# Vision tower on one core: who prepares the constants between embedding and the first attention pass

## The reference, cut to what matters

```python
def fake_quant(x, n_bits=8):
    qmax = 127
    scale = max(max(abs(x)) / qmax, 1e-8)      # one scale for the whole tensor
    return clip(round(x / scale), -128, 127) * scale
h = tokens(x)                                   # 64 x 197 x 192
y = layernorm(h)
qkv = fake_quant(y) @ fake_quant(w_qkv).T + b_qkv
attn = softmax(fake_quant(q) @ fake_quant(k).T * 16 ** -0.5)
out = fake_quant(attn) @ fake_quant(v)
h = h + fake_quant(out) @ fake_quant(w_proj).T + b_proj
h = h + experts(layernorm(h))
```

## Time and profile before

| What | us |
|---|---|
| median of 3 runs (lowest, highest) | 2035.22 (2034.53, 2038.62) |
| the profiled execution, its own time | 2038.77 |
| its span | 2037.0 |
| busy: PE / DVE / ACT / POOL | 1492.0 / 1433.1 / 1379.6 / 1164.9 |
| prologue of `normalise`, first instruction to `turn(1)` | 285.56 to 311.72 |
| loop of `normalise` | 311.72 to 422.6 |
| epilogue and barrier | 422.65 to 428.9 |
| start of `attend_maxima` to its first matmul | 428.91 to 435.21 |

### The profile page before, as it was taken

How to read it: one execution, slowest core, us unless ns; L and a number is a source line. 1 busy time by engine, 2 the same in 40 slices (tenths; PEclk the granted TensorE clock), 3 DMA queues, 4 the chain that set the end, 5 groups by cost and what they waited for, 6 DMA issues and landing times. The chain is left out here.

```text
span 2037.0 us, 50049 instructions
## 1 busy us (share of the span) xinstructions
PE 1492.0 (73%) x12152; PEld 987.7 (48%) x12153; DVE 1433.1 (70%) x3551; ACT 1379.6 (68%) x3956; POOL 1164.9 (57%) x1903
## 2 busy tenths in 40 slices
PE   6999957855656556563688885888864999994563
PEld 6999954411111111111344443554434988884553
DVE  2545559977777777777466666888876777774996
ACT  1323224429999999997799995777662766663885
POOL 2333330046666666663356552577775788884997
PEclk9999978965555555555555555555556999996886
DMA  7654410002222222221554545444434555554785
GB/s 293 256 233 191 163 39 1 1 28 87 83 74 74 76 86 81 76 74 52 124 151 138 151 139 153 137 155 154 151 120 116 134 139 144 145 145 143 224 270 158
DMA packets 184912, 262.77 MB, mean 129 GB/s; under 512 B 28372, under 2 KB 147363, under 8 KB 180328
## 3 DMA queue, kind: packets, MB, share of 16 engines
q1 hardware_dynamic: 137456, 202.16, 32.0%
q0 software_dynamic: 19840, 39.17, 5.4%
q10 hardware_dynamic: 27540, 20.52, 3.1%
HBM read 149.17 MB, written 108.01 MB: 126 GB/s over the span
## 5 line engine op out<-in xcount | busy, mean ns | idle before, releaser
L947 ACT ACTIVATE exps_summed<-s,neg_shift 128x197 f32<-128x197 f32 x1184 | 482.7, 479 | 33.9 <-POOL neg_shift L814 32.7
L984 DVE TENSOR_REDUCE score_max<-s 128x788 f32 (+2 forms) x320 | 284.7, 893 | 107.7 <-PE s L888 95.0
L947 ACT ACTIVATION_READ_ACCUMULATOR exps_summed<-s,neg_shift (+1 forms) x1184 | 304.9, 260 | 0.0
L1346 ACT ACTIVATE exps<-st,scalars 128x788 f32<-128x788 f32 (+1 forms) x320 | 246.4, 889 | 15.4 <-PE st L1255 15.4
L2027 POOL DMA_INDIRECT expert_sums<-y_tile,row_places x216 | 215.5, 998 | 60.3 <-issue 25.6
L367 PE MATMUL mm<-w_tok,x_transposed 128*128 128x192 f32 x1176 | 209.5, 329 | 0.8 <-ACT x_transposed L328 0.8
L888 PE MATMUL s<-k_int,qk_int 16*128 16x197 bf16 x768 | 98.8, 355 | 138.6 <-ACT exps_summed L947 123.4
L328 ACT COPY x_transposed<-tp 128x768 f32<-128x768 f32 x98 | 78.1, 798 | 176.9 <-PE tp L359 176.9
L367 PEld LDWEIGHTS mm<-w_tok,x_transposed 128*128 128x128 f32 x1176 | 190.9, 192 | 1.2 <-ACT x_transposed L328 1.2
L350 POOL TENSOR_SCALAR x_patches<-x_tile 128x768 f32<-128x768 f32 x98 | 81.4, 831 | 188.0 <-PE tp L359 172.2
L1166 POOL TENSOR_SCALAR probs<-exps 128x788 bf16<-128x788 f32 (+1 forms) x160 | 130.0, 819 | 102.5 <-ACT exps L1346 102.4
(11 more groups left out here) (416 smaller groups left out, 4506.1 us busy)
## 6 DMA issues: line engine op xcount, KB each, us to landing
x_tile<-in_x SPq DMA_DIRECT2D x21, 1792.0 KB, 11.0
z_tile<-listed_rows SPq DMA_DIRECT2D x108, 196.0 KB
v_ints<-v_slots SPq DMA_DIRECT2D x32, 480.0 KB
v_slots_in<-v_ints SPq DMA_DIRECT2D x32, 480.0 KB, 3.7
q_ints<-qk_int SPq DMA_DIRECT2D x32, 295.5 KB
k_ints<-k_int SPq DMA_DIRECT2D x32, 295.5 KB
q_shifted<-q_ints SPq DMA_DIRECT2D x32, 295.5 KB, 3.6
k_ones<-k_ints SPq DMA_DIRECT2D x32, 295.5 KB, 4.2
```

Source lines behind the costliest of these rows:

```text
L947: act.activation(gone[:, v % 2, k], ps[v % 3][:, k, 0:SEQ], ACT.Exp, scale=alpha, bias=nb[:, s, to:to + 1], accum_out=p.lsum[:, bass.ds(n ...
L984: dve.tensor_reduce(columns(m, u), src, op=ALU.max, axis=AXL.X).then_inc(max_done, 1)
L1346: act.activation(ex[:, v % 4, 0:size(u)], src, ACT.Exp, scale=alpha, bias=p.col(C_LNSA)).then_inc(e_ready, 1)
```

## The change

1. POOL takes over, behind its fill of ones in `normalise`: the six instructions on the bias row (after waiting for `rows_ok` and the loads), then, after `b_mv` and a new semaphore `cw_ok`, the five copies of weight slots, the two broadcasts into `kk`, and the four clears that stood at the start of `attend_maxima`.
2. The six maxima of the weights (L559 to L564) move behind the rows' chain on DVE.
3. The sum that gives `C_ONES` moves from the epilogue to the start of DVE's stream.
4. PE runs `turn(0)` ahead of the transposes of the weights, DVE runs `spread(0, 0)` ahead of the copies out of PSUM, and PE waits for `b_mv` itself before the loop.
5. `masks` counts to 3 and `zero` to 1. The five tiles are allocated outside of `attend_maxima`.

```diff
@@ normalise, gpsimd
                 pool.memset(x1[D1:KB], 1.0).then_inc(ones_ok, 1)
                 pool.wait_ge(ones_ok, 1)
+                link = make_link(pool, bch)
+                pool.wait_ge(rows_ok, 1)
+                pool.wait_ge(ld, 80)
+                link(pool.tensor_scalar(brow[:], brow[:], p.col(C_IX, 0, 1), p.col(C_IW, 0, 1), ALU.mult, ALU.mult))
+                link(pool.tensor_copy(bpart[:, 0], brow[:]))
+                link(pool.tensor_tensor(bres[:], brow[:], bpart[:, 0], ALU.subtract))
+                link(pool.tensor_copy(bpart[:, 1], bres[:]))
+                link(pool.tensor_tensor(bres[:], bres[:], bpart[:, 1], ALU.subtract))
+                link(pool.tensor_copy(bpart[:, 2], bres[:]))
+                pool.sem_inc(b_in, 1)
+                pool.wait_ge(b_mv, 48)
+                pool.wait_ge(cw_ok, 1)
+                for to, w in ((p.wslot0, cw0), (p.wslot1, cw1)):
+                    for t in range(2):
+                        link(pool.tensor_copy(to[:].rearrange("p g a w -> p (g a) w")[:, :, HD * t:HD * t + HD],
+                                              w[:, t * D:(t + 1) * D].rearrange("p (s d) -> p s d", d=HD)))
+                link(pool.tensor_copy(p.wv0[:], cw0[:, 2 * D:3 * D]))
+                for k in range(2):
+                    pool.tensor_copy(p.kk[:, k].rearrange("p g t -> p (g t)"),
+                                     p.col(C_ONES).broadcast_to([128, GRP * 2 * SEQ])).then_inc(laid, 1)
+                for v in (p.lq, p.xl0, p.xl1, p.vs):
+                    pool.memset(v[:], 0.0).then_inc(laid, 1)
+                pool.wait_ge(laid, 6)
@@ normalise, tensor
                 spread_maxima(nc, p, bank, 3, red)
+                def turn(t):
+                    ...
+                turn(0)
                 pe.wait_ge(w_ok, 1)
...
-                turn(0)
                 pe.wait_ge(w_ok, 2)
                 pe.wait_ge(ones_ok, 1)
+                pe.wait_ge(b_mv, 48)
@@ normalise, vector
                 link(dve.memset(mx[:], 0.0))
+                slots = p.idf[:].rearrange("p (h s) -> p h s", s=SLOT)
+                link(dve.reduce_sum(p.col(C_ONES), slots[:, :, HD:HD + 3], axis=AXL.XY))
...
-                dve.wait_ge(ld, 80)
-                (six maxima of the weights)
                 dve.wait_ge(chain_a, 2)
                 (the rows' chain)
+                dve.wait_ge(ld, 80)
+                (six maxima of the weights)
                 dve.sem_inc(max_ok, 1)
...
-                dve.sem_inc(w_ok, 1)
-                (six instructions on the bias row)
-                dve.sem_inc(b_in, 1)
-                dve.wait_ge(w_t, 1)
-                (six copies out of PSUM)
-                dve.wait_ge(b_mv, 48)
-                (five copies into slots)
                 dve.sem_inc(w_ok, 1)
+                spread(0, 0)
+                dve.wait_ge(w_t, 1)
+                (six copies out of PSUM)
+                dve.sem_inc(cw_ok, 1)
+                dve.sem_inc(w_ok, 1)
@@ attend_maxima
-                sp.wait_ge(masks, 5)
+                sp.wait_ge(masks, 3)
...
-                pool.memset(lq[:], 0.0).then_inc(zero, 1)
-                pool.memset(xl0[:], 0.0).then_inc(zero, 1)
-                pool.memset(xl1[:], 0.0).then_inc(zero, 1)
                 pool.tensor_copy(na[:], p.col(C_NALPHA).broadcast_to([128, 4])).then_inc(zero, 1)
-                pool.memset(vs[:], 0.0).then_inc(zero, 1)
-                pool.wait_ge(zero, 5)
-                pool.wait_ge(masks, 5)
+                pool.wait_ge(zero, 1)
+                pool.wait_ge(masks, 3)
...
-                for s in range(2):
-                    dve.tensor_copy(kk[:, s].rearrange("p g t -> p (g t)"),
-                                    p.col(C_ONES).broadcast_to([128, GRP * 2 * SEQ])).then_inc(masks, 1)
-                dve.wait_ge(masks, 5)
+                dve.wait_ge(masks, 3)
```

More of the change, by code:

```diff
@@ L432, in normalise @@
         (ld, chain, chain_a, red, w_t, w_ok, b_in, b_mv, y_ready, t_done, x_ready, cls_t,
-         q_done, q_max, red2, eps_ok, max_ok, rows_ok, ones_ok, tick_t) = p.sems(
+         q_done, q_max, red2, eps_ok, max_ok, rows_ok, ones_ok, cw_ok, laid, bch, tick_t) = p.sems(
             p.early, "b", "ld chain chain_a red w_t w_ok b_in b_mv y_ready t_done x_ready cls_t "
-            "q_done q_max red2 eps_ok max_ok rows_ok ones_ok tick_t")
+            "q_done q_max red2 eps_ok max_ok rows_ok ones_ok cw_ok laid bch tick_t")
         DOUBLES = ([((q, j), (q, j + 1)) for q in range(PAIRS) for j in (0, 2)]
@@ L489, in _ @@
                 spread_maxima(nc, p, bank, 3, red)
+                def turn(t):
+                    b = t % 2
+                    pe.wait_ge(y_ready, t + 1)
+                    need(pe, x_ready, t - 1)
+                    for u in range(2):
+                        nc.tensor.transpose(pa[b][:, u, 0:ROWS], y[:, b, u, 0:128], p.idf[0:ROWS, 0:ROWS])
+                        done = nc.tensor.transpose(pa[b][0:D1, 2 + u, 0:ROWS], y[:, b, u, 128:D], p.idf[0:ROWS, 0:ROWS])
+                    done.then_inc(t_done, 1)
+                turn(0)
                 pe.wait_ge(w_ok, 1)
@@ L504, in _ @@
                 last.then_inc(w_t, 1)
[L506 to L513, removed]
                 def channels(g, d):
@@ L578, in _ @@
                 link(dve.tensor_tensor(pm[0:ROWS, 0:1], pm[0:ROWS, 0:1], cst[0:ROWS, 11:12], ALU.max))
+                dve.wait_ge(ld, 80)
+                link(dve.tensor_reduce(pm[:, 1:2], w_rows[:, 0:4, :], op=ALU.max, axis=AXL.XY, apply_absolute_value=True))
+                link(dve.tensor_reduce(cst[0:64, 12:13], w_rows[0:64, 4, :], op=ALU.max, axis=AXL.X, apply_absolute_value=True))
+                link(dve.tensor_tensor(pm[0:64, 1:2], pm[0:64, 1:2], cst[0:64, 12:13], ALU.max))
+                link(dve.tensor_reduce(pm[:, 2:3], w_tail[:, 0, :], op=ALU.max, axis=AXL.X, apply_absolute_value=True))
+                link(dve.tensor_reduce(cst[0:64, 13:14], w_tail[0:64, 1, :], op=ALU.max, axis=AXL.X, apply_absolute_value=True))
+                link(dve.tensor_tensor(pm[0:64, 2:3], pm[0:64, 2:3], cst[0:64, 13:14], ALU.max))
                 dve.sem_inc(max_ok, 1)
@@ L637, in spread @@
                     ins.then_inc(x_ready, 1)
+                spread(0, 0)
+                dve.wait_ge(w_t, 1)
+                pw = pq[:].bitcast(BF16)
+                link(dve.tensor_copy(cw0[:], pw[:, 0, 0:3 * D]))
+                link(dve.tensor_copy(cw1[0:D1, :], pw[0:D1, 1, 0:3 * D]))
+                link(dve.tensor_copy(p.wp0[:], pw[:, 2, 0:D]))
+                link(dve.tensor_copy(p.wp1[0:D1], pw[0:D1, 3, 0:D]))
+                link(dve.tensor_copy(x0[:, :, 0:1], pw[:, 4, 0:1].rearrange("p (a b) -> p a b", a=1).broadcast_to([128, B, 1])))
+                link(dve.tensor_copy(x1[0:D1, :, 0:1], pw[0:D1, 4, 128:129].rearrange("p (a b) -> p a b", a=1).broadcast_to([D1, B, 1])))
+                dve.sem_inc(cw_ok, 1)
+                dve.sem_inc(w_ok, 1)
                 def maxima(g, d):
@@ L647, in _ @@
                     for w2 in range(SIDE // 2):
-                        spread(g, w2)
+                        if g or w2:
+                            spread(g, w2)
                         if g:
@@ L905, in scores @@
                     ins.then_inc(s_ready, 1)
-                pe.wait_ge(masks, 5)
+                pe.wait_ge(masks, 3)
                 for g in range(GRP):
@@ L2391, in build @@
             p.cw1 = far("w_qkv1", [KB, 3 * D], BF16)
+            p.kk = far("k_int", [128, 2, GRP, 2 * SEQ], BF16)
+            p.lq = far("q_ends", [128, 2, 2, GRP * STAMP], BF16)
+            p.xl0 = far("x_ends0", [128, 2, 256], BF16)
+            p.xl1 = far("x_ends1", [KB, 2, 256], BF16)
+            p.vs = far("v_slots", [128, 2, VW], BF16)
             normalise(p)
```

14 lines of the change are left out of this document (1 added, 13 removed).

## The result

| kernel | median us (lowest, highest) | against before, 95% interval |
|---|---|---|
| before, 4 runs beside it | 2035.42 (2034.53, 2038.62) | |
| after, 4 runs | 2050.08 (2049.00, 2050.62) | 1.0063 [1.0050, 1.0076] |

The change costs about 14.7 us where 4.3 us of gain were forecast; the time lies outside the range of 2026 to 2034 and on the other side of the old kernel.

The account below looks back on a forecast made before the run. Gains were sought around the normalisation's DVE-busy loop: DVE's chain ahead, PE waiting for DVE's broadcasts behind. 5.9 us behind less 1.6 ahead gave 4.3; 2035.22 - 4.3 = 2030.9 us, range 2026 to 2034.

Parts of the forecast that it names:

- The later stages start at barriers and shift as a whole.: Stages behind the first attention pass: the 4.3 us gain was to carry through to the kernel's end.
- D: Rival, normalisation loop: POOL's work holds DVE's spreads, making the kernel slower, up to 2040 us; chance 6%.
- Masks and clears: Behind the normalisation loop: PE starts attention 5.7 us sooner and the late sum saves 0.2 us, 5.9 in all.
- Held by the fill: Prologue: POOL's fill holds L199 until 296.16, leaving 0.86 of 2.26 us; row factors at 298.34 instead of 299.20.
- Bias: Prologue: POOL's bias work takes turns with DVE's rounding, which ends at 307.25 instead of 303.51.
- cheap bound: Prologue: POOL's first bias instruction priced from 0.68 us instead of 1.8; rounding ends at 306.15, gain 5.4 us.
- turn(1): PE's step at the end of the prologue: starts at 313.3 instead of 311.72, 1.6 us later.
- The added wait for: PE ahead of the normalisation loop: bias lands at 309.0, so the wait costs nothing, with 4 us of cover.
- C: Rival, prologue: POOL stalls at first use, so PE's bias wait comes last; gain 2.5 us, 2032.7; chance 17%.
- POOL's slots, broadcasts and clears in the loop: Normalisation loop: some 9.5 us of POOL work costs zero; up to 9 us if that fails.
- A: The forecast: DVE and POOL take turns in the prologue; gain 3 to 6 us, 2029.2 to 2032.2; chance 62%.
- Local sum: Normalisation: 5.9 us gained behind the loop less 1.6 lost ahead of it, 4.3 us.

Follow-up runs that it names:

- Experiments 1 and 2: experiment 1, and the kernel before with 28 embedding row maxima taken in pairs, 14 DVE instructions fewer: 2055.55 us, ratio 1.0086.
- experiment 1: The kernel after with 14 one-column memsets on DVE ahead of its first wait in the embedding: 2033.94 us, ratio 0.9986.
- -14: DVE's projection loop 14 places earlier than before: the kernel after, 2050.08 us, and the kernel before with 14 DVE instructions fewer, 2055.55 us.
- +114: The kernel before with 114 one-column memsets on DVE in the embedding, loop 114 places later: 2055.53 us.
- -20: The kernel after with 12 embedding row maxima taken in 6 pairs, loop 20 places earlier than before: 2036.25 us.
- -11: The kernel after with 3 one-column memsets on DVE in the embedding, loop 11 places earlier than before: 2033.98 us.
- -7: The kernel after with 7 one-column memsets on DVE in the embedding, loop 7 places earlier than before: 2036.24 us.
- 0: DVE's projection loop at its old place: the kernel before, 2035.42 us, and the kernel after with 14 memsets, 2033.94 us.

## Why the prediction was wrong

The step that failed is its last one: "The later stages start at barriers and shift as a whole." They start at barriers, but the time that they take isn't fixed if the instructions ahead of them have changed in number. Taking 14 instructions off DVE's stream was counted by their durations alone; it also moved the projection's loop onto a bad place, at 22.0 us in that stage. Experiments 1 and 2 show that this count alone switches the loss off and on. None of the rivals had it: D, the slower one, sat in the normalisation (POOL holding spreads), and L637's spreads there last 431 to 478 ns (432 to 476 before), with DVE as busy in the loop as before (78.38 against 78.46).

The other steps, against the trace:

- *Masks and clears:* 5.7 + 0.2 foreseen behind the loop; the loop ended 0.44 later and PE started 5.48 sooner, 5.92.
- *Held by the fill:* L199 was to end at 296.2, it ended at 296.08; row factors at 298.34 foreseen, at 298.22 found.
- *Bias:* the first instruction was taken at 1.8 us from its nearest row (L753) and took 0.81. With it the rounding was to end at 307.25; with the cheap bound, 306.15. It ended at 305.93. Here the size was off, not the mechanism. The waiting was DVE's almost alone, though (3.4 us of it against 0.4 on POOL).
- *turn(1):* 1.6 later foreseen with the dear price, 0.5 with the cheap one, 0.38 found.
- *The added wait for* `b_mv`*:* not last; PE's idle before `turn(1)` was ended by DVE's `w_ok`. C falls.
- *POOL's slots, broadcasts and clears in the loop:* free within 0.2 us, as in A (its maxima last 100.9 us against 100.7).
- *Local sum:* 4.3 foreseen (5.4 cheap), 5.5 found up to the attention's first matmul.
- *A small loss that is open:* from the first to the last summed exponential the first attention pass takes 507.5 us before, 508.8 after and 508.4 to 509.6 in the other kernels with the early start, so 4.2 of the 5.5 arrive at the projection. I tested no cause for it.

With a good place the mechanics of A give what they promised: the kernel of experiment 1 gains 2.9 us by its ratio, interval 0.8 to 5.1, against the 4.3 of the forecast.

## What to carry to other kernels

Count the instructions of each engine in every hardware loop. Here a loop of 260 on DVE was at a bad place at 2 of the 6 distances tried, and its version of 252 at the same place was not. Any edit ahead of such a loop that changes the number of instructions, even one that removes work, can put it there. So compare the instruction packets and the waits on "issue" at the loop's first line before a slowdown is laid to the edit. And where two engines hold each other off, put the work of the one that has time behind the other's critical stretch, not beside it.

## What the runs showed of the hardware that was not expected

- At a bad place of its loop DVE stops for 6.3 to 6.8 us at each jump back, while five pieces of 8192 bytes are read on average; four jumps cost the stage 22 us. This was so at two places 128 instructions apart (-14 and +114), not at -20, -11, -7 and 0.
- DVE's rounding and POOL's bias instructions beside each other cost DVE 3.4 us and POOL 0.4 us.
- An engine with a backlog takes up part of another's stall: of the 17.8 us by which DVE's last rows came later, POOL's backlog left 13.4.
- POOL's TENSOR_SCALAR with two pointer scalars took 0.81 us for 576 values on one partition in both kernels shown, 1.4 ns an element, less than half of what L753 suggests (1275 ns for 394).
